# Half-width state in the first and last step of an eight-expert LSTM tower

## The reference, cut to what matters

```python
mask = (top_idx.T[:, None, :] == arange(E)[None, :, None])        # K = 2 choices, E = 8 experts
expert_x = (mask[..., None] * flat_x).reshape(K, E, S, B, I)      # zero rows where not chosen
def step(carry, xt):                                              # for each k and e, over S = 16 steps
    h, c = carry                                                  # both start at zero
    gates = xt @ Wi + h @ Wh + b
    i_, f_, g_, o_ = split(gates, 4)
    c = sigmoid(f_) * c + sigmoid(i_) * tanh(g_)
    h = sigmoid(o_) * tanh(c)
    return (h, c), h @ Wo + bo
y = einsum('ken,nk,keno->no', mask, rw, out)                      # only chosen outputs are summed
```

## Time and profile before

| | |
|---|---|
| median of 3 runs | 1681.88 us (1679.94 to 1682.21) |
| profiled execution, time | 1681.96 us |
| its span, first to last instruction | 1680.2 us |
| mean granted TensorE clock | 0.988 |
| TensorE matmul busy | 1576.4 us (94%) |
| VectorE busy | 1524.8 us (91%) |
| ScalarE busy | 887.0 us (53%) |
| GpSimd busy | 49.5 us (3%) |

### The profile page before, as it was taken

How to read it: one execution, slowest core, us unless ns; L and a number is a source line. 1 busy time by engine, 2 the same in 40 slices (tenths; PEclk the granted TensorE clock), 3 DMA queues, 4 the chain that set the end, 5 groups by cost and what they waited for, 6 DMA issues and landing times.

```text
span 1680.2 us, 21553 instructions
## 1 busy us (share of the span) xinstructions
PE 1576.4 (94%) x7416; PEld 757.3 (45%) x7416; DVE 1524.8 (91%) x2440; ACT 887.0 (53%) x1004; POOL 49.5 (3%) x43
## 2 busy tenths in 40 slices
PE   7767999999999999999999999999999999999998
PEld 3433444444444444444444444444444444444443
DVE  5578999999999999999999999999999999999876
ACT  4256545454554655545465554545546555454554
POOL 1000000000000000000000000000000000000000
PEclk8898999999999999999999999999999999999999
DMA  4133535344454454545446354454534445364452
GB/s 138 22 84 109 154 115 162 124 124 145 132 155 121 140 137 130 148 120 144 136 129 159 115 162 127 120 146 133 154 120 141 136 131 150 118 149 130 151 154 66
DMA packets 254766, 219.75 MB, mean 131 GB/s; under 512 B 131429, under 2 KB 174360, under 8 KB 254657
## 3 DMA queue, kind: packets, MB, share of 16 engines
q1 hardware_dynamic: 254576, 218.36, 45.5%
q10 hardware_dynamic: 80, 0.02, 0.0%
HBM read 73.06 MB, written 4.74 MB: 46 GB/s over the span
## 4 chain that ended last, share of the span: by engine, by line
PE 52%; DVE 36%; issue 8%; ACT 2%; DMA 1%; SPq 1%; POOL 0%; DVEq 0%; ACTq 0%
PE gates L584 14%; PE gates L583 14%; PE gates L578 11%; DVE C L1094 4%; DVE tmp L1118 4%; PE yp L590 3%; DVE H L1087 3%; DVE C L1122 3%; DVE H L1101 2%; DVE tmp L1111 2%; PE FA L523 2%; DVE z L1131 2%; PE FA L508 2%; ACT tmp L747 1%; DVE pr L966 1%
## 5 line engine op out<-in xcount | busy, mean ns | idle before, releaser
L747 ACT ACTIVATE tmp<-gates,bias_sb 128x1024 f32<-128x1024 f32 x504 | 558.5, 1111 | 505.2 <-PE gates L584 489.4
L584 PE MATMUL gates<-H,wh_sb 128*128 128x512 f32 x960 | 490.2, 592 | 0.0
L583 PE MATMUL gates<-H,wh_sb 128*128 128x512 f32 x960 | 490.2, 592 | 0.0
L578 PE MATMUL gates<-xm,wi_sb 128*128 128x512 f16 x1512 | 411.5, 381 | 6.4 <-ACT tmp L747 4.4
L584 PEld LDWEIGHTS gates<-H,wh_sb 128*128 128x128 f32 x960 | 182.4, 190 | 229.6 <-issue 229.6
L578 PEld LDWEIGHTS gates<-xm,wi_sb 128*128 128x128 f16 x1512 | 143.6, 99 | 282.6 <-issue 191.6
L754 ACT ACTIVATE tmp<-C 128x1024 f32<-128x1024 f32 x128 | 135.3, 1057 | 171.0 <-DVE C L1122 167.3
L583 PEld LDWEIGHTS gates<-H,wh_sb 128*128 128x128 f32 x960 | 182.3, 190 | 69.1
L1111 DVE SCALAR_TENSOR_TENSOR tmp<-tmp 128x1024 f32<-128x1024 f32 x120 | 145.2, 1210 | 36.2 <-ACT tmp L747 35.7
L1094 DVE COPY_PREDICATED C<-masks,Cx 128x1024 f32<-128x1024 uint16 x120 | 158.6, 1321 | 1.5 <-DMA Cx<-C 1.5
L1101 DVE SCALAR_TENSOR_TENSOR H<-tmp 128x1024 f32<-128x1024 f32 x128 | 155.9, 1218 | 2.1 <-ACT tmp L754 2.1
(11 more groups left out here) (167 smaller groups left out, 1246.2 us busy)
## 6 DMA issues: line engine op xcount, KB each, us to landing
Hx<-H SPq DMA_DIRECT2D x240, 256.0 KB, 2.6
Cx<-C SPq DMA_DIRECT2D x240, 256.0 KB, 2.4
masks<-mask_scratch SPq DMA_DIRECT2D x128, 256.0 KB, 5.1
roww<-mw_scratch SPq DMA_DIRECT2D x128, 256.0 KB, 3.4
diag<-pr SPq DMA_DIRECT2D x64, 112.0 KB, 3.1
diag<-vwin SPq DMA_DIRECT2D x64, 112.0 KB, 3.1
out_dram<-h SPq DMA_DIRECT2D x16, 256.0 KB, 2.7
C<-in_wi SPq DMA_DIRECT2D x1, 2048.0 KB, 10.8
```

Of the source, the lines that this page charges most:

```text
L578: mm(fed, wi_sb[:, e, wpart, rows_of], xm[:, e % 2, vpart, :], start=(wpart == HI and vpart == HI), stop=(first and wpart == LO))
L583: mm(fed, wh_sb[:, e, rows_of], H[:, e, 0:SEQ], start=False, stop=True)
L584: last = mm(other, wh_sb[:, e, rows_of], H[:, e, SEQ:2 * SEQ], start=True, stop=True)
L747: A(tmp[:, gate_at(gate, e), :], gates[:, (n - 1) % 2, :], ACT.Tanh, bias=bias_sb[:, e, gate:gate + 1], scale=UNSCALE).then_inc(s_tanh, 1)
```

## The change

The states of step 0 in the other half depend on the biases alone, because input and state are zero there. And after the last step nobody reads the other half. So gates, tanh, cell, exchange and state are now worked on the fed 512 columns only in steps 0 and 15 (`width(s)`). In step 15 the exchange still reads the other half of the state before, so one crosswise DMA of the two stays and the predicated copies have half their width. The zero matmul of step 0 goes, and with it the memset of its operand on GpSimd. The other half's first state is worked out from `bias_sb` for all experts at once, on 128x8 tiles (one tanh of the biases and one of the cell on ScalarE, two small operations on VectorE), and ScalarE copies it into the 512 columns of each expert: 8 copies into `C` at unit 7 and 8 into `H` at unit 12 of the part before step 0. SP waits for these 16 copies before the exchanges of step 1.

```diff
+        def width(s):
+            return SEQ if s in (0, STEPS - 1) else K * SEQ
+        def copies_to(s, e):
+            n, full = (s - 1) * E + e + 1, (STEPS - 2) * E
+            return 16 * (K * min(n, full) + max(0, n - full))
...
             def copy_c(s, e):          # copy_h alike
-                for k in range(K):
+                if s == 1:
+                    sp.wait_ge(s_fill, 2 * E)
+                for k in range(width(s) // SEQ):
                     sp.dma_start(Cx[:, k * SEQ:(k + 1) * SEQ], C[:, e, (1 - k) * SEQ:(2 - k) * SEQ]).then_inc(s_c_copy, 16)
...
-                if first:
-                    last = mm(other, wi_sb[:, e, HI, rows_of], zero_in, start=True, stop=True)
-                else:
-                    mm(fed, wh_sb[:, e, rows_of], H[:, e, 0:SEQ], start=False, stop=True)
+                if not first:
+                    last = mm(fed, wh_sb[:, e, rows_of], H[:, e, 0:SEQ], start=False, stop=True)
+                if width(s) > SEQ:
                     last = mm(other, wh_sb[:, e, rows_of], H[:, e, SEQ:2 * SEQ], start=True, stop=True)
...
-                A(tmp[:, gate_at(gate, e), :], gates[:, (n - 1) % 2, :], ACT.Tanh, bias=bias_sb[:, e, gate:gate + 1],
+                A(tmp[:, gate_at(gate, e), 0:width(s)], gates[:, (n - 1) % 2, 0:width(s)], ACT.Tanh, bias=bias_sb[:, e, gate:gate + 1],
                   scale=UNSCALE).then_inc(s_tanh, 1)
-                A(tmp[:, TANH_C, :], C[:, e, :], ACT.Tanh, scale=0.5).then_inc(s_tc, 1)
+                A(tmp[:, TANH_C, 0:width(s)], C[:, e, 0:width(s)], ACT.Tanh, scale=0.5).then_inc(s_tc, 1)
...
+            def fill_other(dst, i):
+                for e in range(E):
+                    A(dst[:, e, SEQ:2 * SEQ], state0[:, i, e:e + 1].to_broadcast([P, SEQ]), ACT.Copy).then_inc(s_fill, 1)
...
                 if t == ACT_AT["h"]:
                     split_wi_hi()
+                    A(bias_t[:, :, :], bias_sb[:, :, :], ACT.Tanh).then_inc(s_state0, 1)
                 if t == ACT_AT["summary"]:
                     scale_wh()
+                    act.wait_ge(s_state0, 2)
+                    A(state0[:, 1, :], state0[:, 0, :], ACT.Tanh, scale=0.5).then_inc(s_state0, 1)
+                if t == ACT_AT["window"]:
+                    act.wait_ge(s_wlo, 3)
+                    fill_other(C, 0)
+                if t == ACT_AT["feature"]:
+                    act.wait_ge(s_state0, 4)
+                    fill_other(H, 2)
...
                 if t == DVE_AT["xn"]:
                     split_wi_lo()
+                    dve.wait_ge(s_state0, 1)
+                    STT(out=state0[:, 0, :], in0=bias_t[:, :, I], scalar=1.0, in1=bias_t[:, :, G],
+                        op0=ALU.add, op1=ALU.mult).then_inc(s_state0, 1)
+                if t == DVE_AT["w_out"]:
+                    dve.wait_ge(s_state0, 3)
+                    STT(out=state0[:, 2, :], in0=bias_t[:, :, O], scalar=1.0, in1=state0[:, 1, :],
+                        op0=ALU.add, op1=ALU.mult).then_inc(s_state0, 1)
...
-            G_.memset(H[:, E - 1, 0:SEQ], 0.0).then_inc(s_hzero, 1)
```

More of the change, by code:

```diff
@@ L130, in lm_tower_kernel @@
         lab = sb("lab", [P, TILES, E])
+        bias_t = sb("bias_t", [P, E, 4])
+        state0 = sb("state0", [P, 3, E])
         mkw = pr[:, 256:256 + TILES * (WT0 + E)].rearrange("p (t e) -> p t e", t=TILES)
@@ L218, in lm_tower_kernel @@
         s_wh = sem("s_wh")
-        s_hzero = sem("s_hzero")
+        s_state0 = sem("s_state0")
+        s_fill = sem("s_fill")
         s_c_copy = sem("s_c_copy")
@@ L237, in lm_tower_kernel @@
         s_enc_out = sem("s_enc_out")
-        s_czero = sem("s_czero")
         s_mask_in = [sem("s_mask_in0"), sem("s_mask_in1")]
@@ L456, in _ @@
             zeros = xnT[:, :].bitcast(f16)
-            zero_in = H[:, E - 1, 0:SEQ // 2].bitcast(f16)
             pe.wait_ge(s_warm, 1)
@@ L577, in unit_gate @@
                 for wpart, vpart in ((HI, HI), (HI, LO), (LO, HI)):
-                    mm(fed, wi_sb[:, e, wpart, rows_of], xm[:, e % 2, vpart, :], start=(wpart == HI and vpart == HI),
-                       stop=(first and wpart == LO))
-                if first:
-                    last = mm(other, wi_sb[:, e, HI, rows_of], zero_in, start=True, stop=True)
-                else:
-                    mm(fed, wh_sb[:, e, rows_of], H[:, e, 0:SEQ], start=False, stop=True)
+                    last = mm(fed, wi_sb[:, e, wpart, rows_of], xm[:, e % 2, vpart, :],
+                              start=(wpart == HI and vpart == HI), stop=(first and wpart == LO))
+                if not first:
+                    last = mm(fed, wh_sb[:, e, rows_of], H[:, e, 0:SEQ], start=False, stop=True)
+                if width(s) > SEQ:
                     last = mm(other, wh_sb[:, e, rows_of], H[:, e, SEQ:2 * SEQ], start=True, stop=True)
@@ L640, in _ @@
             pe.wait_ge(s_wohalf, 1)
-            pe.wait_ge(s_hzero, 1)
             run_steps(step)
@@ L1079, in masked_input @@
                 TT(xm[:, e % 2, :, :], xs[:, par, :, :], mv_, ALU.mult).then_inc(s_xm, 1)
-            halves = lambda ap: ap.rearrange("p (k t) -> p k t", k=K)
+            halves = lambda ap: ap.rearrange("p (k t) -> p k t", t=SEQ)
             def swap_h(s, e):
[L1085 to L1088, removed]
+                dve.wait_ge(s_h_copy, copies_to(s, e))
+                w = width(s)
+                V.copy_predicated(halves(H[:, e, 0:w]), masks[:, e % 2, 1:2, :].to_broadcast([P, w // SEQ, SEQ]).bitcast(u16),
+                                  halves(Hx[:, 0:w])).then_inc(s_h_swap, 1)
             def swap_c(s, e):
[L1092 to L1095, removed]
+                dve.wait_ge(s_c_copy, copies_to(s, e))
+                w = width(s)
+                V.copy_predicated(halves(C[:, e, 0:w]), masks[:, e % 2, 1:2, :].to_broadcast([P, w // SEQ, SEQ]).bitcast(u16),
+                                  halves(Cx[:, 0:w])).then_inc(s_c_swap, 1)
             def hidden(s, e):
@@ L1100, in hidden @@
                 dve.wait_ge(s_tanh, gates_to(s, e, 3))
-                STT(out=H[:, e, :], in0=tmp[:, gate_at(O, e), :], scalar=1.0, in1=tmp[:, TANH_C, :],
+                w = width(s)
+                STT(out=H[:, e, 0:w], in0=tmp[:, gate_at(O, e), 0:w], scalar=1.0, in1=tmp[:, TANH_C, 0:w],
                     op0=ALU.add, op1=ALU.mult).then_inc(s_h, 1)
@@ L1105, in input_part @@
                 dve.wait_ge(s_tanh, gates_to(s, e, 1))
-                at_i, at_g = tmp[:, gate_at(I, e), :], tmp[:, gate_at(G, e), :]
+                at_i, at_g = tmp[:, gate_at(I, e), 0:width(s)], tmp[:, gate_at(G, e), 0:width(s)]
                 if first:
-                    STT(out=C[:, e, :], in0=at_i, scalar=1.0, in1=at_g,
+                    STT(out=C[:, e, 0:SEQ], in0=at_i, scalar=1.0, in1=at_g,
                         op0=ALU.add, op1=ALU.mult).then_inc(s_c, 1)
@@ L1116, in cell @@
                 dve.wait_ge(s_c_swap, s * E + e - E + 1)
-                at_f = tmp[:, gate_at(F, e), :]
-                STT(out=at_f, in0=at_f, scalar=1.0, in1=C[:, e, :],
+                w = width(s)
+                at_f = tmp[:, gate_at(F, e), 0:w]
+                STT(out=at_f, in0=at_f, scalar=1.0, in1=C[:, e, 0:w],
                     op0=ALU.add, op1=ALU.mult).then_inc(s_v, 1)
@@ L1121, in cell @@
                 dve.wait_ge(s_u, s * E + e - E + 1)
-                STT(out=C[:, e, :], in0=at_f, scalar=0.5, in1=tmp[:, gate_at(I, e), :],
+                STT(out=C[:, e, 0:w], in0=at_f, scalar=0.5, in1=tmp[:, gate_at(I, e), 0:w],
                     op0=ALU.mult, op1=ALU.add).then_inc(s_c, 1)
```

## The result

The changed kernel takes 1644.42 us (median of 4 runs, 1643.80 to 1644.77) against 1681.53 us (1679.94 to 1682.21) beside it: a ratio of 0.9783 [0.9772, 0.9795]. That is 37.1 us less where 32.7 were forecast. The profiled execution took 1644.5 us with a span of 1642.7 us at a mean granted clock of 0.988; the spans differ by 37.5 us.

The account below looks back on a forecast made before the run. TensorE was taken to pace the middle and last steps, chains of work step 0. Last step 28.6 + step 0 4.8 - before step 0 0.7 = 32.7 us, so 1682.0 - 32.7 = 1649.3 us, range 1645 to 1656 (own 1647 to 1652).

Parts of the forecast that it names:

- Last step, matmuls: Step 15: 0.86 us less TensorE time in each of 31 gates ahead of the last chain, 26.7 us gained.
- the 0.5 us for a slot of `gates`: Start of step 15: expert 0's F gate waits some 0.5 us for a slot; 0.5 (0 to 2) taken off.
- Tail: After the last F gate of step 15: a shorter chain of operations takes 3.8 us, which gains 2.4 us.
- Step 0: Shrinking operations on step 0's chain of waits, less what paths beside it take back: 4.8 us gained, bounds 1 and 8.8.
- four paths beside it: Step 0: expert 3's mask, projection transpose, router operations and next embedding's copy take back 1.0, 1.2, 0.9 and 0.9 us.
- The first deduction: Step 0: expert 3's mask, issued behind unmoved DMAs, lets its `xm` come at most 0.9 us earlier, not 1.9: -1.0.
- the other three paths: Step 0: projection transpose (-1.2), router's small operations on VectorE (-0.9) and next embedding's copy (-0.9) limit the gain.
- Before step 0: Part before step 0: table load and bias tanh make `xnT` 0.6 us late, a small VectorE operation 0.1: -0.7 us.
- Step 0 gives nearly nothing: Rival: step 0, held by DMA landings, the front or a lower TensorE clock, gives 1 us; 1653.1 us; chance 0.17.
- Last step paced by an exchange or a mask: Rival: an exchange or mask, not TensorE, paces step 15 at 8.5 us an expert, losing 13 us; 1662 us; chance 0.09.
- Table reloads: Rival: first Tanh's table lacks Exp, so ScalarE reloads 8 times a step over 15 steps; 1726 us; chance 0.02.
- The whole chain: Rival: step 0 gives its whole chain, 8.8 us or more, as waits beside it start earlier; 1645.3 us; chance 0.08.

Follow-up runs that it names:

- last_pe_full: The changed kernel with the other half's fp32 gate matmul worked again on TensorE in step 15, all else there narrow: 1671.5 us, ratio 0.9953 to the kernel before.
- last_only: The kernel before with the narrow state in step 15 alone; step 0 and everything ahead of it unchanged: 1649.55 us, ratio 0.9825.
- experiment 3: Changed kernel's step 0: repeated unchanged 1643.05 us; with its zero matmuls back 1644.18 us; with these and full-width ScalarE tanhs 1647.94 us.
- tail_warm: The kernel before with 14 bf16 filler matmuls in TensorE's last wait: 1681.12 us, ratio 1.0006.
- zero_back: The changed kernel with the 24 zero matmuls of step 0 put back: 1644.18 us, ratio 0.9780 to the kernel before.
- later_tail_zero: The changed kernel with bias tanh and table load later, 8 filler matmuls in TensorE's last wait and step 0's zero matmuls back: 1643.95 us, ratio 0.9785.
- tanh_later: The changed kernel with bias tanh and table load behind the first attention unit's copies, the small VectorE operation also later: 1643.13 us, ratio 0.9774.
- fill_twice: The changed kernel with eight more 128x512 copies behind the first eight, into the fed half of `H`: 1646.92 us, ratio 0.9796.
- first_only: The changed kernel with step 15 in full width again, so narrow in step 0 alone: 1674.24 us, ratio 0.9968 to the kernel before.
- last_rest_full: The changed kernel with everything in step 15 wide again except TensorE, which still skips the other half's matmul: 1662.27 us, ratio 0.9899.

## Why the prediction fell short by 4.8 us

- **Last step, matmuls: right.** 26.7 us forecast for 31 gates; gate distance, full TensorE and last_pe_full show it.
- **Last step, the 0.5 us for a slot of `gates`: wrong.** TensorE starts the first F gate of step 15 at 1580.84 without it, right behind the tanh of the I gate, which ends at 1580.70. The narrow `swap_h` of the first expert (0.73 us, at 1575.34) already lies in the end of step 14, ahead of the full-width cell on VectorE that ScalarE waits for there. I had left it full width; the 0.6 us that it saves are about what I took off. This is read from the order of the trace and was not tested. The bias matmul of the output, L610, which waited 0.45 us before, starts at 1592.93 without a wait. Together 26.96 instead of 26.2.
- **Tail: operations right, clock missed.** Of 3.25 us, 2.45 are from operations (2.4 forecast) and 0.8 from TensorE's pieces: 1.14 + 0.67 us instead of 1.48 + 1.13. It is no certain gain: last_only, with the same tail, had 1.27 and 1.13 us.
- **Step 0: the failed step.** I took 4.0 us off the chain's 8.8 for four paths beside it. In the profiled pair the gain, measured from the second `qT`, is 3.6 us already at the projection's transpose and 6.3 where the next embedding is copied. The first deduction took the mask's issue as fixed, but it came 0.56 us earlier, and its `xm` followed 5.05 us behind it, not 6.5. In both traces that `xm` stands behind other work of VectorE without idle time, so the mask did not hold it. For the other three paths my reading, not tested, is that they start from operations that had themselves moved. As an upper bound the chain's rows held: 6.3 of 8.8 us, so 2.5 us were to be taken off, not 4.0. By experiment 3 they belong elsewhere than I put them. Up to `h_sb` the zero matmuls give 0 net (1.5 in the chain), the tanhs 1.8 to 2.1 (3.0), and VectorE the rest, 4.2 to 4.7 (4.3). The parts were undone in one order only, so VectorE's share is what was left over.
- **Before step 0: mechanism right, net wrong.** `xnT` was forecast 0.6 us late and is 0.56 late behind `h_sb`. In the pair `h_sb` itself started 0.29 us later, and from `xnT` to the second `qT` it took 56.59 us against 57.71, which more than pays for both. TensorE had a higher granted clock there, from 60 to 70 us:

```profile
60.00:65.00 5.00, 4.00 (x66) 1.99 (x61) 2.80 (x8) 1.91 (x4) 0.00 (x0) 0.72 0.00 0
65.00:70.00 5.00, 3.89 (x19) 1.84 (x19) 2.96 (x13) 0.28 (x1) 1.38 (x1) 1.00 0.00 0
```

  Before, both stretches have 0.50. The six other runs whose part before step 0 is that of the changed kernel took 56.6 to 57.7 us from `xnT` to the second `qT`, last_only and tail_warm 57.7 and 58.0: so the 1.1 us come and go with the execution, and a forecast has no claim to them. The Trainium skill (ScalarE: Activation LUTs, "What ACT_TABLE_LOAD costs") has a drain of 1.38 us behind each load; the trace disagrees, with 0.01 us between the load and the tanh at 31.91.
- **Rivals.** "Step 0 gives nearly nothing" fell by 6.3 us. "Last step paced by an exchange or a mask" fell: TensorE is full, with masks landing 4.9 us after their issue and `Hx` 4.2. "Table reloads" fell: two loads in all. "The whole chain" named the nearest time (1645.3 us) with too large a step 0: its 8.8 us were 6.3 to 6.9, and the last step and the start made up the rest.

## What to carry to other kernels

Price a saved operation from the engine that is full, but look whether the next engine stays under the new pace: here 14 to 15 of 30 us came only because TensorE's work and that of VectorE and ScalarE were halved together. On a chain of waits, don't take a parallel path as fixed until its own first instruction is shown not to move, and don't count short matmuls between two waits as gain when their going lowers the clock as well. When a few tenths are at stake, compare stretches from one instruction to another, and cover what is added with idle time read from the row it precedes, as the eight copies in 5.12 us.

## What the runs showed of the hardware

**A clock drop in a full stretch.** From step 2 on, middle steps take 101.8 to 102.1 us each in every run (from one step's `qT` to the next), but one in tail_warm, one in zero_back and two in later_tail_zero took 103.70. In tail_warm (first fence) it can be seen beside the same place of the step in the kernel before, which lies 1.75 us later (second fence):

```profile
1452.00:1462.00 10.00, 10.00 (x32) 5.10 (x31) 7.18 (x20) 3.92 (x6) 0.00 (x0) 0.83 0.43 130
```

```profile
1453.75:1463.75 10.00, 10.00 (x36) 5.16 (x35) 8.85 (x21) 4.36 (x6) 0.00 (x0) 1.00 0.42 130
```

TensorE is busy for 10.00 of 10 us in both, at a granted clock of 0.83 in tail_warm, a mixture of 2.4 and 1.2 GHz: from 1452 to 1454 us it is 0.50. TensorE had been idle for 1.91 us ahead of 1451.04, and for 1.88 us at the same place in the kernel before, where the clock stays at 1.00. Why it falls in some stays open.

**The tail's clock is not settled by the idle time alone.** With some 2 us idle ahead of it, the last output matmul took 1.14 us in four runs, but 1.27, 1.81, 1.87 and 1.60 in four others (last_only, tanh_later, fill_twice, last_pe_full). With 3.6 us idle it took 1.48 (before) and 1.14 (first_only), with 4.5 us 2.09 (last_rest_full). With fillers it took 1.14 in all three.

**What a lower clock costs depends on where it falls.** Step 0 of tanh_later took 63.84 us, from the second `qT` to the first fp32 gate matmul, at a granted clock of 0.87, and that of zero_back 64.00 at 0.95. The changed kernel's profiled execution, at 0.84, took 65.64: 1.3 us more than the 9.1 of others lie in its last 10.4 us, with the clock at 0.67 and TensorE busy for 9.39 us. Over the whole step TensorE is busy for 45 to 50 us in the narrow runs and waits for others in the rest.
